# Hundreds of steps moved by a few places in five engine orders, and 50 bank choices changed

## The reference

```python
x = layernorm(x + mamba(x))          # per sequence: in_w, conv over 4 taps, silu, dt, a scan
                                     # over 256 tokens with 16 states for each of 256 channels,
                                     # y = sum of states * C + D*u, times silu(gate), out_w
x = layernorm(x + ffn(x))            # two layers, each on its own shift_token(x):
  q, k, v = split(h @ wqkv)          #   8 heads of 64; l2norm, scale and rotary on q and k
  o = local_attention(q, k, v)       #   windows of 64, own and previous window, softmax
  x = x + o @ wo
  h = layernorm(shift_token(x))*lg + lb
  a, g = split(h @ w1 + b1)          #   341 + 341 columns, in chunks of 128, 128 and 85
  x = x + (a * gelu(g)) @ w2 + b2
```

## Time and profile before

| what | value |
|---|---|
| median of three runs | 1025.17 us |
| lowest and highest | 1023.71 and 1028.51 us |
| the profiled execution, its own time | 1025.69 us |
| its span from first to last instruction | 1023.9 us |
| mean granted TensorE clock | 0.979 |
| busy share PE, DVE, ACT, POOL | 89%, 87%, 77%, 68% |

### The profile page before, as it was taken

One profiled execution on the slowest core, in us unless ns is written; L12 is line 12 of the kernel. 1 busy time (PEld: TensorE's weight loads), 2 busy tenths in 40 slices (PEclk: granted clock), 3 DMA queues, 4 the chain that ended last, 5 costly groups with the idle time before them and its releaser, 6 DMA issues. The chain is left out here.

```text
span 1023.9 us, 26019 instructions
## 1 busy us (share of the span) xinstructions
PE 906.2 (89%) x10152; PEld 550.7 (54%) x10152; DVE 890.3 (87%) x1244; ACT 788.3 (77%) x1901; POOL 701.1 (68%) x386
## 2 busy tenths in 40 slices
PE   3767678999988898999899989999899999999985
PEld 1333335456455465646564555546565566676664
DVE  7798997999879997999899998999899997774643
ACT  4467766996888859977898759995987987778771
POOL 4062424998579984799588892999478497886651
PEclk9979889999999999999999999999999999999998
DMA  7000000000001100000101100100110000010000
GB/s 239 11 17 16 12 1 21 23 19 15 17 17 27 27 23 16 18 22 22 32 18 27 22 12 22 28 23 6 28 32 23 2 23 22 17 33 18 17 22 11
DMA packets 22618, 25.63 MB, mean 25 GB/s; under 512 B 2869, under 2 KB 14815, under 8 KB 22495
## 3 DMA queue, kind: packets, MB, share of 16 engines
q1 hardware_dynamic: 22207, 23.81, 9.0%
q10 hardware_dynamic: 288, 0.14, 0.0%
HBM read 9.26 MB, written 2.10 MB: 11 GB/s over the span
## 5 line engine op out<-in xcount | busy, mean ns | idle before, releaser
L1088 DVE TENSOR_TENSOR_SCAN scan<-du,decay 128x1028 f32<-128x1028 f32 (+1 forms) x160 | 315.0, 2004 | 2.8 <-issue 1.3
L793 POOL TENSOR_TENSOR rn<-ssc,expo 128x16 f32<-128x16 f32 x64 | 214.6, 3354 | 5.3
L884 ACT ACTIVATE decay<-delta,negA 128x1024 f32<-128x1024 f32 (+1 forms) x160 | 154.9, 997 | 43.3 <-DVE scan L1088 37.7
L1278 PE MATMUL YY<-scan,diag 64*64 64x512 f32 (+1 forms) x1280 | 148.1, 552 | 32.1 <-DVE scan L1088 31.7
L789 POOL TENSOR_SCALAR ssc<-ss 128x16 f32<-128x16 f32 x64 | 61.9, 967 | 152.7 <-DVE ss L1145 152.0
L798 POOL TENSOR_TENSOR qkc<-qkc,qks 128x1024 f32<-128x1024 f32 x64 | 163.0, 2547 | 0.5 <-DVE qks L1163 0.3
L802 POOL TENSOR_TENSOR qkc<-qkc,rn 128x1024 f32<-128x1024 f32 x64 | 143.5, 2242 | 5.0
L940 ACT ACTIVATE prob<-AA,nmax 128x128 f32<-128x128 f32 x240 | 84.5, 384 | 15.1 <-DVE nmax L1183 15.0
L940 ACT ACTIVATE prob<-BB,nmax 128x128 f32<-128x128 f32 x232 | 81.7, 381 | 17.3 <-DVE nmax L1183 14.9
L1145 DVE TENSOR_REDUCE ss<-sq 128x16 f32<-128x1024 f32 x64 | 77.2, 1206 | 15.1 <-ACT sq L903 15.1
L1278 PEld LDWEIGHTS YY<-scan,diag 64*64 64x64 f32 x1280 | 38.3, 139 | 94.5 <-DVE scan L1088 68.9
(11 more groups left out here) (210 smaller groups left out, 2279.2 us busy)
## 6 DMA issues: line engine op xcount, KB each, us to landing
v_even<-v_odd SPq DMA_DIRECT2D x96, 128.0 KB, 2.3
x<-in_x SPq DMA_DIRECT2D x6, 256.0 KB, 3.3
wqkv<-in_wqkv SPq DMA_DIRECT2D x1, 1536.0 KB
xT<-in_xT SPq DMA_DIRECT2D x6, 256.0 KB, 2.7
out<-outb SPq DMA_DIRECT2D x6, 256.0 KB, 2.3
w<-in_w SPq DMA_DIRECT2D x1, 682.0 KB
xT<-in_xT SPq DMA_DIRECT2D x4, 128.0 KB, 2.5
x<-in_x SPq DMA_DIRECT2D x4, 128.0 KB, 2.9
```

Source lines behind the costliest of these rows:

```text
L793: pool.tensor_tensor(rn[:, q % 2, :], ssc[:, :], expo[:, 0:2 * HEADS], ALU.pow).then_inc(rn_sb, 1)
L884: act.activation(decay[:, at % A_RING, both(g), 1:], delta[:, both(g), :], ACT.Exp, scale=negA[:, n:n + 1]).then_inc(decay_sb, 1)
L1088: dve.tensor_tensor_scan(state, step, a, 0.0, ALU.add, ALU.mult).then_inc(scan_sb, 1)
L1278: return pe.matmul(dst, lhsT, rhs, start=start, stop=stop, skip_group_check=True)
```

## The change

No operation, buffer or semaphore is added or removed. In the five orders steps trade places with steps near them. Counted as the steps outside the longest common subsequence of the two lists, 207 of 848 change their place on PE, 139 of 654 on ACT, 154 of 710 on DVE, 18 of 197 on POOL and 15 of 89 on SP; the farthest are 6 places on PE, 9 on ACT and POOL, 14 on DVE (`tables 0`) and 7 on SP. In the tables 22 of the letters for pairs change (none for `qk_in`) and 28 letters for single banks; for `up_a` they are those of `up_a 2 1`, `up_a 9 0` and `up_a 11 0`, for `up_gate` those of 3 and 9 and the pair of 18, for `v_in` those of 1, 4, 10 and 35.

How many steps of a name stand at an earlier and at a later position in their list:

| engine | step, earlier / later |
|---|---|
| PE | `qk_T` 25 / 8, `scores` 20 / 9, `qk_in` 19 / 10, `up_a` 18 / 10, `norm_T` 9 / 1, `attn_out` 6 / 1, `v_in` 19 / 20, `out_T` 16 / 18, `weighted` 12 / 20, `state_y` 35 / 55 |
| DVE | `scan` 46 / 18, `sums` 24 / 12, `row_max` 23 / 10, `hidden` 20 / 7, `attn_sum` 9 / 2, `mamba_sum` 4 / 0, `final_stats` 2 / 5, `final_out` 2 / 6, `inverse` 14 / 38 |
| ACT | `qk_T` 18 / 12, `softmax` 12 / 6, `squares` 16 / 11, `gelus` 3 / 0, `layer_T` 4 / 7, `decay` 33 / 41 |
| POOL | `scale` 14 / 1, `rotate` 9 / 2, `mamba_rstd` 5 / 1, `final_rstd` 2 / 4, `residual` 3 / 6 |
| SP | `v_even` 16 / 9, `load_x` 3 / 1, `load_xT` 3 / 3, `store` 1 / 4 |

The full diff replaces nearly all lines of the orders. Below are the places that the text speaks of, with the lines broken at the steps concerned instead of at the file's width.

```diff
 PE_ORDER
-v_in 1, qk_in 1, rank 1, step_in 1, skip 1,
+qk_in 1, rank 1, step_in 1, v_in 1, skip 1,
...
-up_gate 2, probs_T 10, up_a 2 0, up_a 2 1,
+up_gate 2, up_a 2 0, probs_T 10, up_a 2 1,
...
-state_y 4 0, qk_in 15, out_T 11, probs_T 12, v_in 14,
+out_T 11, qk_in 15, probs_T 12, v_in 14, state_y 4 0,
...
-state_y 4 4, v_in 16, scores 14, up_gate 3, up_a 3 0, up_a 3 1, state_y 4 5, up_a 3 2,
+v_in 16, scores 14, up_gate 3, up_a 3 0, state_y 4 4, up_a 3 1, up_a 3 2, state_y 4 5,
...
-weighted 15, state_y 4 11, up_gate 4, up_a 4 0, up_a 4 1, state_y 4 12, out_T 15, up_a 4 2,
-probs_T 16, state_y 4 13, down 4, weighted 16, qk_T 17, qk_in 19, state_y 4 14, scores 17,
+up_gate 4, weighted 15, up_a 4 0, up_a 4 1, state_y 4 11, up_a 4 2, probs_T 16, qk_T 17,
+out_T 15, qk_in 19, state_y 4 12, weighted 16, down 4, scores 17, state_y 4 13, state_y 4 14,
...
-out_T 17, rank 5, v_in 20, scores 19, weighted 18,
+out_T 17, v_in 20, scores 19, rank 5, weighted 18,
...
-weighted 21, state_y 5 5, scores 22, up_a 6 0, state_y 5 6, up_a 6 1,
+state_y 5 5, scores 22, up_a 6 0, weighted 21, up_a 6 1,
...
-state_y 6 12, state_y 6 13, out_T 31, probs_T 32,
+out_T 31, state_y 6 12, state_y 6 13, probs_T 32,
...
-mamba_out 6, out_T 32, v_in 35, norm_T 9, qk_T 34,
+out_T 32, v_in 35, mamba_out 6, norm_T 9, qk_T 34,
...
-v_in 36, qk_in 36, rank 7, up_a 9 1, up_a 9 2,
+qk_in 36, up_a 9 1, rank 7, v_in 36, up_a 9 2,
 DVE_ORDER
-differences 0, masks 0, step_size 0, tables 0, scan 0 0, scan 0 1,
+masks 0, step_size 0, differences 0, scan 0 0, scan 0 1,
...
-scan 0 13, scan 0 14,
+scan 0 13, tables 0, scan 0 14,
...
-scan 4 0, ffn_stats 3, attended 11,
+scan 4 0, attended 11, ffn_stats 3,
 POOL_ORDER
-scale 11, residual 2, mamba_rstd 3, rotate 11,
+mamba_rstd 3, scale 11, rotate 11, residual 2,
 SP_ORDER
-store 1, v_even 19, load_xT 6, v_even 20, v_even 21, v_even 22, v_even 23, load_x 6, v_even 24, v_even 25,
+v_even 19, v_even 20, load_x 6, v_even 21, v_even 22, store 1, v_even 23, v_even 24, v_even 25, load_xT 6,
 PAIR_TABLES, BANK_TABLES (letters that change: number, before, after)
-"up_gate" 3 M, 9 M    "up_a" 2 1 C, 9 0 M, 11 0 C    "v_in" 35 C    "scores" 53 B, 55 B, 58 A
+"up_gate" 3 C, 9 C    "up_a" 2 1 M, 9 0 C, 11 0 M    "v_in" 35 M    "scores" 53 Y, 55 A, 58 B
```

More of the change, by code:

```diff
@@ L95 @@
[L95 to L134, removed]
@@ new lines @@
+1, state_y 2 2, scores 2, qk_T 3, weighted 1, state_y 2 3, state_y 2 4, state_y 2 5, state_y 2 6, state_y 2 7,
+probs_T 2, out_T 1, weighted 2, state_y 2 8, attn_out 0, state_y 2 9, state_y 2 10, scores 3, shift 0, state_y 2 11,
+state_y 2 12, probs_T 3, state_y 2 13, state_y 2 14, state_y 2 15, norm_T 0, out_T 2, up_gate 0, up_a 0 0, mamba_out
+2, weighted 3, u_in 3, out_T 3, up_a 0 1, gate_in 3, layer_T 0 2, up_a 0 2, qk_in 4, v_in 4, rank 3, qk_in 5,
+step_in 3, v_in 5, down 0, attn_out 1, qk_T 4, qk_in 6, layer_T 1 0, scores 4, v_in 6, skip 3, shift 1, state_y 3 0,
@@ new lines @@
+v_in 41, qk_in 41, up_a 10 2, scores 39, state_y 7 10, weighted 38, down 10, probs_T 39, qk_T 40, out_T 38, state_y
+7 11, weighted 39, scores 40, state_y 7 12, qk_in 42, out_T 39, state_y 7 13, attn_out 11, probs_T 40, v_in 42,
+state_y 7 14, qk_T 41, weighted 40, shift 11, state_y 7 15, out_T 40, scores 41, qk_in 43, mamba_out 7, v_in 43,
+u_in 8, norm_T 11, gate_in 8, qk_T 42, layer_T 0 7, probs_T 41, up_gate 11, scores 42, weighted 41, qk_in 44, up_a
+11 0, up_a 11 1, up_a 11 2, rank 8, out_T 41, step_in 8, probs_T 42, v_in 44, down 11, qk_T 43, weighted 42, v_in
@@ new lines @@
+12, qk_T 47, gate_in 9, up_a 12 0, up_a 12 1, up_a 12 2, rank 9, qk_in 49, step_in 9, scores 47, weighted 46, down
+12, qk_T 48, skip 9, qk_in 50, state_y 9 0, state_y 9 1, out_T 46, probs_T 47, layer_T 0 8, state_y 9 2, state_y 9
+3, v_in 50, scores 48, state_y 9 4, state_y 9 5, weighted 47, state_y 9 6, v_in 51, out_T 47, probs_T 48, attn_out
+13, qk_T 49, qk_in 51, scores 49, shift 13, weighted 48, state_y 9 7, state_y 9 8, out_T 48, state_y 9 9, probs_T
+49, v_in 52, state_y 9 10, qk_T 50, weighted 49, norm_T 13, scores 50, state_y 9 11, up_gate 13, state_y 9 12,
@@ L229 @@
[L229 to L232 removed]
+u_in 1, layer_T 0 0, squares 0, silu_gate 1, v_in 0, silu_u 1, rank 1, squares 1, softplus 1, decay 1 0, decay 1 1,
```

430 lines of the change are left out of this document (227 added, 203 removed).

## The result

| kernel | median, us | range, us |
|---|---|---|
| before | 1026.84 | 1023.71 to 1029.07 (4 runs) |
| changed | 1047.14 | 1046.0 to 1047.37 (4 runs) |

The ratio is 1.0198, with a 95% interval of 1.0165 to 1.023: clearly slower, by 1.7 to 2.3%. I had forecast 1017.4 us and given 0.20 to slower; the time lies outside the range, which went up to 1032. It is near the 1044.7 us of rival A paid in full.

A forecast was written before the change was run, and what follows sets the result against it. PE, the tighter, and DVE were taken to bind together. Clean repairs -1.9, fillers -9.4 and bank debits +3.5 summed to -7.8 us, from 1025.2 to 1017.4 us; likeliest case 1009 to 1020, 8 in 10 from 1002 to 1032.

The forecast's parts named there:

- rival A: PE steps put ahead of their inputs stall everything behind: 1034.3 us half paid, 1044.7 paid in full; chance 0.14.
- DVE's fillers: inverse, final_stats and final_out mostly go later on DVE; 62% of 15.1 us credited, -9.4 us.
- steps that trade places: PE steps swapped ahead of one stall reach it at the same time, so the wait mostly stays; 0 us.
- What bounds the kernel: From 200 to 950 us PE and DVE bind together, PE tighter; only PE's idle 43.2 us can change, or DVE's instructions lengthen.
- Clean repairs: PE waits at up_a 4 1 and up_a 9 2 get covered by ready work; -1.9 us together.
- Debits of the banks: PE waits on just-used banks at v_in 35, v_in 20, up_a 3 0 and up_a 2 1; +3.5 us.
- The beginning: First 200 us: tables 0 and v_in 1 go later, the same DVE work stands before scan 0 14; 0 us.
- SP: load_x 6 goes ahead of v_even 21, whose copy still lands before weighted 21 needs it; 0 us.
- Rival D: DVE's long scans meet POOL's work more often and lengthen, +7.9 us, giving 1031.7 us; chance 0.06.

The follow-up runs named there:

- clean_repairs: The kernel before with four stretches of the change on PE alone (17 steps, with their letters); 1031.65 us (1.0055).
- final_late: The kernel before with 17 final_stats and final_out steps two places later on DVE, nothing else; 1040.17 us (1.0141).
- both_undone: The changed kernel with its moves and letters of 205 to 290 and 540 to 630 us put back on PE, ACT, DVE and POOL; 1037.39 us (1.0101).
- twenty_swaps: The kernel before with 20 randomly drawn pairs of neighbours on PE swapped; 1042.17 us (1.0137).
- weighted_back: The changed kernel with 19 of its 20 later weighted steps on PE put as many places earlier; 1070.2 us (1.041).

## Why the prediction was wrong

The step that failed is the sum: it adds prices of single moves, each read from the trace of before with all other times held fixed. Two of its terms failed most, the -9.4 us for DVE's fillers, which gave the forecast its sign, and the 0 for steps that trade places, where two waits alone cost 5.7 us. The terms one by one:

**What bounds the kernel** was read rightly: PE and DVE together, with dozens of short waits. The conclusion from it, that the change "can only give or take part of PE's 43.2 us", was wrong. PE's own work grew by 8.4 us, 6.2 of them in the steps at the three waits followed by a lower clock. And two engines that wait for each other can idle in turn: PE's idle time rose by 13.0 us and DVE's by 31.5 (133.6 to 165.1).

**Clean repairs (-1.9).** The two waits are gone in the changed kernel, as forecast: neither `up_a 4 1` nor `up_a 9 2` waits. The step that failed is to count them as gains: in `clean_repairs` both are gone too, and together with two stretches like them they cost 5.4 us.

**DVE's fillers (-9.4).** "Have nobody waiting soon" is not true. `softmax` of tile q+2 waits for `inverse q`, which frees the row sums that it adds up (2.1 us of wait before, 8.3 in the changed kernel). `ffn_sum 4` waited 2.01 us in `final_late` for the store behind `final_out`. And the price of 0.457 us for one `final_out` instruction is a mean that hides two cases, 1.07 and 4.86 us for four. Nor does anything tie the 62%, a share of PE's waits, to the moved work. Tested alone in the kernel before, and in a larger dose, what I had credited cost 15 and 14 us; in the first DVE's instructions became 11.0 us longer and ACT's wait for the reciprocal 5.1. In the changed kernel the sign is the other one: there the later `inverse` are worth 12.7 us. So these moves have no price of their own that could stand in a sum, and what they are worth within the whole change stays open.

**Debits of the banks (+3.5).** Right in kind and about in size, as waits. PE's timeline of the changed kernel at `v_in 20` and `v_in 35`:

```profile
406.20 1.10 PE L1278 MATMUL M<-wqkv,hT 128*128 128x512 f32 x2 [1.52 <-ACT oT L950]
...
624.45 1.10 PE L1278 MATMUL M<-wqkv,hT 128*128 128x512 f32 x2 [0.78 <-ACT oT L950]
```

`v_in 35` waits 0.78 us for ACT's copy, where 0.80 was forecast; `v_in 20` waits 1.52 (0.80) and `up_a 3 0` 1.76 us (0.80); `up_a 2 1` only 0.34 (1.47), as PE came there late. What they cost in time was not tested.

**Steps that trade places in front of the same stall (0).** `state_y 4 0` now waits for nothing, as said, and `out_T 11` waits 1.2 us instead. But at two places PE met a new wait with ready work behind it. `out_T 31` went ahead of two `state_y` and waits 2.57 us. `qk_T 10` keeps its place ahead of `mamba_out 3`, but its input now comes late, and it waits 3.19 us. Two moves gave back 5.7 us.

**The beginning (0).** By 193 us the same work ended 2.9 us later; no run took this apart.

**SP (0).** Right: `weighted 21` waits for nothing. (By the terms given there the copy would land at 438.6 us, not 439.0, and `weighted 21` stands three steps later, not two; both leave it more room.)

**Rival A** has the right sign, part of the mechanism and, by luck, the size. Of the four places that the prediction names as its signs, `up_a 2 1` waits 0.34 us, `out_T 30` not at all, `v_in 35` 0.78 and `scores 56` 0.42. `out_T 31` is a place of its kind (by the trace of before some 1.2 us, 2.57 measured). `qk_T 10`, the dearest, isn't, because its input was late by POOL's chain behind `scale 9` and not by a place in PE's list. The Trainium skill ("PSUM — Partial Sum Buffer", section "Engine vs sequencer instructions") has matmuls start and complete in program order. The trace agrees: `mamba_out 3`, whose input was there at 253.4 us, stands behind `qk_T 10` until 257.01. That rule gave 1044.7 us, 2.4 below the measured time, but not for the reason that it gives: with eleven of the stalls mended about 12 us of loss are left.

**Rival D** is wrong in total and right in place: DVE's busy time fell from 890.3 to 880.2 us, yet single meetings of scans with POOL start the dearest stall. The Trainium skill ("SBUF — State Buffer", section "Who interferes with whom") says that a DVE instruction with two SBUF inputs contends with a GpSimd instruction that reads SBUF. Of DVE's 2-port modes it says that whoever issues first gets the shared ports for the whole instruction and the other is fully blocked. The lengthened rows beside `rotate` agree with such a block, on either side in turn. In `clean_repairs` the second scan begins at 479.06, while POOL's instruction of 477.40 runs until 481.30, and ends at 483.46, 2.2 us after that; a scan alone takes 2.27. `scale` in the changed kernel does not fit the order of issue: begun at 228.63, beside the first scan, it ended only after two more scans that began later (6.61 us).

**What is open.** Some 10 of the 20 us are in neither of the two stretches undone. The trace of `both_undone` spreads them over several places without a fall of the clock, and `twenty_swaps` and `weighted_back` make it likely that they come from any shift of PE against DVE against POOL that lets other instructions meet. That last step is argued, not shown. Which of the 50 letters matter by themselves wasn't tried.
